# High one-hots three steps ahead in eight buffers, and the low one-hot at the end of ScalarE's slot, in a recommender kernel

## The reference

```
ub    = concat(table_i1[his0], table_i2[his1], table_i3[his2])      # 2048 x 200 x 96
h     = concat(q, ub, q - ub, q * ub) @ w_att1.T + b_att1           # q: the row of the item asked for
score = where(his0 == 0, 0, h @ w_att2.T + b_att2)
browse = einsum('bl,ble->be', score, ub)
x = dice(concat(item_emb, browse, user_emb) @ w1.T + b1)
x = dice(x @ w2.T + b2)
out = sigmoid(x @ w3.T + b3)
```

## Time and profile before

| | us |
|---|---|
| median of 3 runs | 1570.45 (1567.71 to 1574.2) |
| the profiled execution | 1565.89 |
| its span, first to last instruction | 1564.1 |
| TensorE busy | 1303.5 (83%) |
| VectorE busy | 1227.8 (78%) |
| ScalarE busy | 1043.1 (67%) |
| GpSimd busy | 1006.5 (64%) |
| first read to last read of the tiles | 47.2 to 1502.2 |
| mean granted TensorE clock | 0.941 of full |

### The profile page before, as it was taken

How to read it: one execution, slowest core, us unless ns; L and a number is a source line. 1 busy time by engine, 2 the same in 40 slices (tenths; PEclk the granted TensorE clock), 3 DMA queues, 4 the chain that set the end, 5 groups by cost and what they waited for, 6 DMA issues and landing times.

```text
span 1564.1 us, 67116 instructions
## 1 busy us (share of the span) xinstructions
PE 1303.5 (83%) x27007; PEld 1205.9 (77%) x27007; DVE 1227.8 (78%) x1143; ACT 1043.1 (67%) x2017; POOL 1006.5 (64%) x1671
## 2 busy tenths in 40 slices
PE   5688979879798887989788897989889798988864
PEld 4577868778797876878788787878878797877861
DVE  6588868777878887887877887787788878889845
ACT  6676667766667775676767666676766767775427
POOL 3577657665767766676765766777576666767630
PEclk8899989989999999999989999999999999999976
DMA  3476666566556667666765666667666566766730
GB/s 54 104 143 131 127 117 131 124 131 135 120 127 145 127 131 125 134 135 113 137 137 128 146 127 123 126 147 126 131 144 130 130 125 141 128 129 155 142 69 1
DMA packets 517516, 194.46 MB, mean 124 GB/s; under 512 B 485445, under 2 KB 493237, under 8 KB 517245
## 3 DMA queue, kind: packets, MB, share of 16 engines
q1 hardware_dynamic: 499654, 162.61, 52.9%
q10 hardware_dynamic: 15448, 26.51, 6.8%
q0 software_dynamic: 2144, 1.36, 0.7%
HBM read 8.45 MB, written 1.44 MB: 6 GB/s over the span
## 4 chain that ended last, share of the span: by engine, by line
POOL 47%; issue 27%; PE 10%; ACT 5%; DVE 4%; DMA 3%; POOLq 2%; ACTq 1%; SPq 0%; DVEq 0%
POOL score L443 17%; POOL score L448 8%; POOL score_r L452 7%; POOL parts L456 4%; PE sel L548 3%; POOL parts L453 3%; POOL parts L449 3%; POOL item_rows L421 3%; PE wsum_ps L565 2%; DMA hiT<-onehot_hi 2%; POOL user_rows L429 2%; ACT scores_b L780 2%; PE misc L661 2%; DVE scaled_lo L1041 1%; DVE score_j L1029 1%
## 5 line engine op out<-in xcount | busy, mean ns | idle before, releaser
L883 ACT ACTIVATE onehot_lo<-sel,one 100x600 bf16<-100x600 f32 x512 | 389.0, 760 | 427.7 <-DVE score_j L1029 417.7
L443 POOL TENSOR_TENSOR score<-score_j 100x16 f32<-100x16 f32 x256 | 363.2, 1419 | 396.0 <-DVE score_j L1029 394.0
L548 PE MATMUL sel<-scoretab,hiT 128*128 128x75 bf16 x12288 | 543.6, 203 | 78.5 <-DMA hiT<-onehot_hi 65.6
L548 PEld LDWEIGHTS sel<-scoretab,hiT 128*128 128x128 bf16 x12288 | 509.8, 101 | 123.4 <-DMA hiT<-onehot_hi 70.7
L1029 DVE TENSOR_REDUCE score_j<-sel 100x24 f32<-100x600 f32 x512 | 398.0, 777 | 220.3 <-PE sel L548 217.4
L1041 DVE TENSOR_TENSOR scaled_lo<-onehot_lo,parts 100x3648 bf16<-100x3648 bf16 x256 | 526.3, 2056 | 15.1 <-POOL parts L456 10.4
L565 PE MATMUL wsum_ps<-scaled_lo,onehot_hi 100*128 100x75 bf16 x12288 | 528.3, 201 | 8.6 <-issue 4.4
L565 PEld LDWEIGHTS wsum_ps<-scaled_lo,onehot_hi 100*128 100x128 bf16 x12288 | 488.2, 100 | 15.4 <-issue 5.6
L1015 DVE TENSOR_TENSOR onehot_hi<-digits,iota_hi 100x1920 bf16<-100x1920 bf16 x256 | 297.8, 1164 | 59.1 <-PE wsum_ps L565 56.1
L780 ACT ACTIVATE scores_b<-acc 128x512 bf16<-128x512 f32 (+1 forms) x318 | 255.4, 803 | 35.3 <-issue 18.2
L773 ACT ACTIVATE wsum_ring<-wsum_ps 128x300 f32<-128x300 f32 x512 | 219.9, 430 | 17.1 <-PE wsum_ps L565 16.5
(11 more groups left out here) (173 smaller groups left out, 760.6 us busy)
## 6 DMA issues: line engine op xcount, KB each, us to landing
scoretab<-scores_b SPq DMA_DIRECT2D x384, 93.8 KB
weightsum<-wsum_ring ACTq DMA_DIRECT2D x128, 125.0 KB
weightsum<-wsum_ring ACTq DMA_DIRECT2D x64, 150.0 KB
raw<-in_r_rec_his_dram SPq DMA_DIRECT2D x32, 150.0 KB
hiT<-onehot_hi SPq DMA_TRANSPOSE x256, 4.0
x_rows<-x_tile SPq DMA_DIRECT2D x14, 100.0 KB
scores_b<-x_rows SPq DMA_DIRECT2D x1, 1400.0 KB
item_rows<-in_L_rec_table_i_dram,ids_now POOLq DMA_INDIRECT x51
```

The source lines that it names most:

```text
L443: pool.tensor_tensor(score_2[:, :], score_j[:, p2, :, 0], score_j[:, p2, :, 1], ALU.add).then_inc(parts_step, 1)
L548: mm = pe.matmul(sel[:, 2 * (s % 2) + q, (c % 4) * W:(c % 4 + 1) * W] .rearrange("p (j v) -> p j v", j=NF), hiT[0:HJ, s // 2 % 4, g * POSP ...
L883: act.activation(onehot_lo[:, n % 2, g0:g0 + 8, 0:W].rearrange("p (q c) u -> p q c u", q=2), sel[0:POS, 2 * (s % 2):2 * (s % 2) + 2, 0:4 * ...
```

## The change

The ring of high one-hots gets eight buffers in place of six, used in plain turn; the wait for a free buffer is then for the sums of the step eight before. AHEAD goes from 2 to 3: VectorE's high one-hot, ScalarE's low rows and SP's transpose of a step are made three steps before its reads, and the prologue makes three of them instead of two. In ScalarE's slot the low one-hot moves from the first place to the last, behind the task's copy, the copy of the weighted sums, the low rows, the collecting DMAs, the digit operations and the split copy of the slot.

```diff
-    RING = 6
+    RING = 8
@@
         def ring_slot(n):
-            return n % 5 if n < STEPS - 1 else RING - 1
-
-        def sums_before(k, n):
-            return 2 * k - (8 if 5 <= n < STEPS - 1 else 10 if n < 5 else 2 * STEPS - 2)
-
-        def ring_used(k, n):
-            return not isinstance(k, int) or sums_before(k, n) > 0
+            return n % RING
+
+        def ring_used(k):
+            return not isinstance(k, int) or k >= RING
@@
-        AHEAD = 2
+        AHEAD = 3
@@ in lo_rows (ScalarE)
-                if ring_used(k, n):
-                    act.wait_ge(wsum_full, sums_before(k, n))
+                if ring_used(k):
+                    act.wait_ge(wsum_full, 2 * (k - RING) + 2)
@@ in slot (ScalarE)
                 here = tasks_of(t)
-                onehot_low(t, s)
@@
                     split_copy(r, stage, SPLIT_DONE * (t + 1) + (3 * r + stage + 1), 1 - odd)
+                onehot_low(t, s)
@@ in onehot_high (VectorE)
-                if ring_used(k, n):
-                    dve.wait_ge(wsum_full, sums_before(k, n))
+                if ring_used(k):
+                    dve.wait_ge(wsum_full, 2 * (k - RING) + 2)
```

## The result

The changed kernel takes 1470.74 us (median of 4 runs, 1465.26 to 1472.56) against 1571.24 before (4 runs): a ratio of 0.9365, 95% interval 0.9328 to 0.9403, so 100 us less. The profiled execution took 1471.44 us with a span of 1469.6, 94.5 less than before. The forecast was 1437, 134 us less.

What follows compares the result with a forecast made beforehand. Bound: a chain of waits between engines, none full. Boundary 5.0 plus split copies 3.4 make 8.4 us a tile, 126 over fifteen, plus 8 in the last: 134 less, 1437 us; 8-in-10 range 1402 to 1515.

Steps and rivals of the forecast that it cites:

- The split slots: Slots with split copies inside a tile: the low one-hot placed last shortens TensorE's waits, booked at 3.4 us a tile.
- the walk: Slot-by-slot shift of ScalarE's instructions in one traced tile: 3.7 of TensorE's 8.2 us split-copy waits go, 4.5 stay.
- the 40 us at which the text would have called itself wrong: Failure sign over the whole run: TensorE's reads wait over 40 us for the low one-hot; up to 10 expected.
- The boundary: Between tiles: an earlier transpose removes TensorE's wait for hiT, gaining 3.4 to 6.2 us a tile, taken as 5.0.
- part 1: Ring of eight, high one-hots three steps ahead: acts at tile boundaries, 5.0 us each over fifteen tiles.
- part 2: Low one-hot at the end of ScalarE's slot: shortens split-copy waits by 3.4 us a tile over fifteen tiles.
- late by its landing: Rival at the boundary: transposes land late even if issued earlier, so the wait stays; 51 us gained, 1520; chance 0.12.
- The low one-hot as the bound: Rival in ScalarE's slots: TensorE waits for the later low one-hot; near no change, or 74 us more, 1645; chance 0.08.
- GpSimd: Rival between pick and scale: GpSimd's operations make scale late, costing 60 us, 1497; mark over 40 us of waits; chance 0.14.
- VectorE's 56.1 us wait: Ahead of VectorE's high one-hot, for TensorE's sums: eight buffers remove it, but nothing booked as gain.
- The first read: Before the first tile: one extra high one-hot, low-row copy and transpose add 0 to 2.8 us.
- The last tile: Final tile, without splits, taking 84.6 us: comes down by 8 us to VectorE's 70.6 plus about 6.

Runs made afterwards that it cites:

- ScalarE's loop written out: Changed kernel with ScalarE's loop over pairs of tiles written out, so that it has no jump back: 1439.4 us, ratio 0.9228 to the kernel before.
- part 2 alone: Kernel before with only the low one-hot moved last in ScalarE's slot, ring of six and AHEAD 2 kept: 1482.0 us, ratio 0.9512.
- Part 1 alone: Kernel before with only the ring of eight and AHEAD 3, low one-hot still first in ScalarE's slot: 1562.3 us, ratio 0.9992.
- the ring alone: Kernel before with only the ring of eight buffers, AHEAD 2 and the low one-hot first kept: 1570.1 us, ratio 1.0043.
- the mid-slot run: Changed kernel with the low one-hot behind the low rows but ahead of collecting DMAs, digit operations and split copy: 1520.5 us, ratio 0.9678.
- and digit operations behind the one-hot: Changed kernel, ScalarE's loop unrolled, digit operations behind the low one-hot in slots 11 and 28, VectorE's maskings in steps 7 and 15: 1416.6 us.
- and gaps in the splits: Changed kernel, loop unrolled, digit operations in slots 12 and 29, no split piece in slots 4 and 22, low one-hot first in 3 and 21: 1418.3 us.

## Why the prediction was right, point by point

**The total** was right in sign and the time lay in the range (1402 to 1515), 34 us above the forecast: three quarters of the gain came. Tiles took 85.0 us on average, where 82 to 85 were named. Between the two profiled executions 94.5 us came of 134. Of the 39.5 that are missing, 39 lie at the boundaries (15 times 5.0 less 2.4), 3 in the last tile and 1.5 in the start; the split slots gave 4 more than booked.

**The split slots**: booked 3.4 us a tile, walked 3.7. Measured 1.9 + 1.8 = 3.7 (slots 3 to 10 and 18 to 25). That it is the walk's own sum is partly luck, for the single sites were less exact. What was walked for slot s of ScalarE falls on TensorE's slot s + 1: slots 4 and 5 gave 1.4 where 1.0 was walked, slot 9 gave 0.4 (0.6), slots 19 and 20 gave 0.7 (0.5), slots 21 and 22 gave 1.2 (0.9), slot 23 took 0.3 where 0.4 was to be gained, slot 24 gave 0.3 (0.3), and slot 18, which the walk left out, took 0.3. Split copies were waited for 59.5 us, where some 70 were named. The low one-hot did become a wait: 39.4 us where up to 10 were expected, each 0.7 at most. That is just under the 40 us at which the text would have called itself wrong.

**The boundary** is the term that was mis-sized: booked 5.0 us, between 3.4 and 6.2; measured 2.4, and 4.2 with ScalarE's loop written out. The step said that the read of slot 0 would start at 961.7 and the pick 3.4 us earlier, and the read did move (slots 31 and 0 lost 4.0 us a tile). The step followed the reads and VectorE's picks over the boundary, but not ScalarE's own list of slots 0 and 1: the item copies, the query matmul behind them, and the jump of the loop. The jump took back 1.9 us a tile on average, 28 us over 15 boundaries, of the 39 that the boundaries fell short. It was to be seen before only as six stands of "issue" ahead of the low one-hot (8.9 us in all) inside a longer wait.

**The parts**: the text gave 75 us to part 1 and 51 to part 2, as if each could be had alone. Measured: 0.1% (within the interval) and 77 to 89 us. So the total was near in part by luck: the change gained 36 us at its boundaries (15 times 2.4), all of it booked to part 1, while part 2 alone gains 22 there (15 times 1.46), which the text had put at nothing. Part 1 alone trades the wait for hiT for one on the item copies. The rival "late by its landing", which left part 2 alone with 1520, was wrong on that number for the same reason: part 2 alone gives 1482.0. In it hiT is waited for 37.0 us, not 65.6; why the boundary read follows its transpose sooner there (one at 990.01 after an issue at 984.30, 5.7 us, where before it was 8.0) stays open.

**Rivals**: late landing did not come, since the wait for hiT is gone altogether. The low one-hot as the bound did not come in the changed kernel, but the run with the digit operations in slots 11 and 28 shows its mechanism: 2.1 us a tile in two slots. Of GpSimd, 19.0 us of waits against the 40 named as the mark, worth some 8 to 12 of the 60 that the rival took.

**Nothings**: the ring alone (1.0043, interval 0.9997 to 1.009) gained nothing, so VectorE's 56.1 us wait was worth nothing. The first read came 1.5 us later (48.7 for 47.2), within the 0 to 2.8; but it came at 48.7 with the ring alone too, which has no extra one-hot ahead of it, so what made it later is not shown. The last tile came down by 4.8 us (its reads start at 1328.39, the last at 1408.2), not 8.

## What to carry to other kernels

When a wait at the border of a loop goes, walk every engine's own list over that border, not only the two engines that met there: here the item copies of a third engine stood one slot behind, and its jump back too. A move of an instruction that waits is worth what stands behind it; to see its price, list both queues, the one that it leaves and the one that it joins. Undo each part alone before crediting it: the part that seemed to bring most brought nothing alone.

## What the runs showed of the hardware

A jump back in ScalarE's loop over two tiles left it standing with nothing to wait for, 3.1 us on average (18.8 us in six), up to 4.4; in the mid-slot run it was 4.7 (28.2 in six), up to 6.1. Written out, the same code ran through. That the stand is the loading of instructions was not tested.

The price of such a stand was higher than its length: TensorE waited 17.3 us, but 31 us of time went with it by the medians (22 by the ratios). The granted clock is part of the price. The record of the granted clock in each trace, from the first read to the last, gives:

```
kernel                                    us at 1.2 GHz   TensorE busy in them
before                                         130               112
part 1 alone                                   131               104
part 2 alone                                    82                72
the change, low one-hot in mid slot            141               122
the change                                      78                69
the change, loop written out                    45                37
 and digit operations behind the one-hot        31                23
 and gaps in the splits                         75                64
```

The 24 matmuls of one read take 1.72 us at this level and 1.01 at the full clock. So, as an estimate, at most half of the right column is lost: up to 21 us of the change's 94.5 between the profiled executions are clock, up to 16 of the loop's 31 and up to 26 of the mid slot's 50, while part 1 alone won back next to nothing.

In all six tiles with a jump TensorE stood 2.2 to 4.1 us ahead of its query matmul, and the low level began between 1.1 us before and 1.8 us after the end of that wait. The Trainium skill (TensorE: Matmul & The Clock Gate, HAM oscillation) describes how a wait lowers TensorE's clock, so that its next work starts cold; the windows agree (0.61 over 3.42 us behind a wait of 2.41 in the change, 0.50 over 3.46 behind 4.21 in part 1 alone).
